# Routing layer of a two-layer conditioned transformer on one core: shared expert parts started two passes earlier, small VectorE steps given to GpSimd

## The reference

```python
# layer 0, pooling
scores = einsum('bsa,a->bs', tanh(hidden @ W1 + b1), v)
p = softmax(where(mask, scores[:, None, :], NEG_INF), -1)
pooled = einsum('bjl,bld->bjd', p, hidden) / mask.sum(-1)[..., None]
# layer 0, routing of the pooled tokens xf
s = softmax(xf @ wg.T)                        # 32 experts in 8 groups
keep_g = the 4 groups with the largest maximum
_, idx = top_k(where(keep_g, s, -inf), 4)
w = take(s, idx);  w = w / (w.sum(-1) + 1e-9)
pos = (cumsum(one_hot(idx), 0) * one_hot(idx)).sum(-1) - 1   # place in the expert
keep = pos < 640
y = scatter_add(w * experts(gather(xf)))
z = (silu(xf @ sw1) * (xf @ sw3)) @ sw2       # the shared expert
x = x + y + z
```

## Time and profile before

| | us |
|---|---|
| median of 3 runs | 1539.36 (1530.76 to 1539.44) |
| profiled execution | 1537.86 |
| its span on the core | 1536.1 |
| TensorE busy in the span | 1402.7 (91%) |
| VectorE busy | 1030.4 (67%) |
| ScalarE busy | 897.8 (58%) |
| GpSimd busy | 654.4 (43%) |

### The profile page before, as it was taken

One profiled execution on the slowest core, in us unless ns is written; L12 is line 12 of the kernel. 1 busy time (PEld: TensorE's weight loads), 2 busy tenths in 40 slices (PEclk: granted clock), 3 DMA queues, 4 the chain that ended last, 5 costly groups with the idle time before them and its releaser, 6 DMA issues.

```text
span 1536.1 us, 27264 instructions
## 1 busy us (share of the span) xinstructions
PE 1402.7 (91%) x9777; PEld 1219.8 (79%) x9777; DVE 1030.4 (67%) x2418; ACT 897.8 (58%) x2092; POOL 654.4 (43%) x624
## 2 busy tenths in 40 slices
PE   7987899999999998789998999998729999999996
PEld 5765799999999997568776776776618998998996
DVE  2998567767777775678887887885435556555552
ACT  5775345545555552268887787788626456455452
POOL 0222344434443414455556666643434445345333
PEclk9997899999999999999999999999759999999998
DMA  5421256666655633557576587575422343234212
GB/s 170 138 83 37 64 152 179 174 163 184 175 169 168 178 98 106 100 96 132 122 141 134 100 131 143 99 123 90 123 85 55 87 108 89 47 92 97 41 22 28
DMA packets 134326, 173.59 MB, mean 113 GB/s; under 512 B 21461, under 2 KB 106272, under 8 KB 134192
## 3 DMA queue, kind: packets, MB, share of 16 engines
q1 hardware_dynamic: 106032, 119.89, 30.4%
q0 software_dynamic: 28160, 51.96, 17.7%
HBM read 107.28 MB, written 42.08 MB: 97 GB/s over the span
## 4 chain that ended last, share of the span: by engine, by line
PE 72%; DVE 9%; issue 6%; DMA 6%; ACT 3%; another core or an unknown queue 2%; POOL 2%; SPq 1%; POOLq 0%; DVEq 0%; ACTq 0%
PE banks L929 45%; PE banks L1437 5%; DMA xe<-pooled,idx 4%; PE banks L1480 4%; PE banks L1533 3%; PE banks L991 3%; PE banks L451 2%; PE banks L1493 2%; PE banks L1454 1%; PE banks L1495 1%; PE banks L1909 1%; PE banks L571 1%; DVE row_at L516 1%; PE banks L1452 1%
## 5 line engine op out<-in xcount | busy, mean ns | idle before, releaser
L929 PE MATMUL banks<-hi_x,hi_w 128*128 128x320 f32 (+1 forms) x832 | 290.7, 349 | 12.1 <-DVE hidden L964 5.2
L929 PE MATMUL banks<-lo_x,hi_w 128*128 128x320 f32 (+1 forms) x832 | 288.1, 346 | 0.0
L929 PE MATMUL banks<-hi_x,lo_w 128*128 128x320 f32 (+1 forms) x832 | 287.6, 346 | 0.0
L929 PE MATMUL banks<-hi_w,hi_h 128*128 128x256 f32 x896 | 261.1, 291 | 2.5 <-DVE X L1018 2.1
L870 POOL DMA_INDIRECT xe<-pooled,idx x160 | 159.2, 995 | 237.4 <-DVE hidden L964 104.3
L929 PE MATMUL banks<-lo_w,hi_h 128*128 128x256 f32 x896 | 253.8, 283 | 0.0
L929 PE MATMUL banks<-hi_w,lo_h 128*128 128x256 f32 x896 | 253.7, 283 | 0.0
L1894 POOL DMA_INDIRECT out<-X,tab x64 | 106.1, 1658 | 190.7 <-DVE X L1997 176.1
L1584 ACT ACTIVATE PN<-banks,smax 128x256 f32<-128x256 f32 (+1 forms) x512 | 180.0, 442 | 12.6 <-DVE smax L1690 12.6
L1410 POOL DMA_INDIRECT got<-done,slot x128 | 126.6, 989 | 133.9 <-DVE smax L1690 70.4
L929 PEld LDWEIGHTS banks<-hi_x,hi_w 128*128 128x128 f32 x832 | 159.9, 192 | 27.3 <-issue 11.0
(11 more groups left out here) (187 smaller groups left out, 2950.7 us busy)
## 6 DMA issues: line engine op xcount, KB each, us to landing
w<-in_L_ffn_w SPq DMA_DIRECT2D x96, 256.0 KB
done<-res SPq DMA_DIRECT2D x32, 640.0 KB
BIG<-in_L_ffn_W SPq DMA_DIRECT2D x16, 1024.0 KB
QS<-parts_qk SPq DMA_DIRECT2D x96, 128.0 KB
KS<-parts_qk SPq DMA_DIRECT2D x96, 128.0 KB
mask<-in_c_masks SPq DMA_DIRECT2D x16, 257.0 KB, 2.8
pooled<-XF SPq DMA_DIRECT2D x16, 256.0 KB, 3.2
WS<-in_L_cond_W SPq DMA_DIRECT2D x16, 256.0 KB
```

What stands on the lines that cost most here:

```text
L929: last = e.matmul(o, a[i], b[j], start=start and k == 0, stop=stop and k == 2, skip_group_check=True)
```

## The change

It does three things. The shared parts' steps stand two passes earlier in the tables of all four engines (`up` of part 0 in TensorE's pass 2 in place of 4, and so on). The second half's one-hot rows (`lane`, half 1) move on VectorE from behind `hit` to the next pass, behind the row maximum `nm` and the `rank` step. And GpSimd takes over from VectorE the pooling's inverse sums (`pool_norm`), the chosen weights (`pool_weigh`) and the running counts (`pool_cum`); with -1 in a new tile `inverse`, the inverse is a power. VectorE's max instruction of the next group and ScalarE's exp of the next group both wait for the chosen weights of the group ahead, which GpSimd now writes. `dve_found` stands at the end of VectorE's list. In layer 1 two loads count on another semaphore; nothing moves there.

```diff
+            if q == 0 and g >= 1 and r.groups:
+                e.wait_ge(r.s_weighted, g)
-        if r.groups:
-            e.tensor_reduce(r.top[:, 0:n], r.tv[:, 0:n, 0:K], AX.X, ALU.add).then_inc(*st.next())
+        if not r.groups:
+            e.reciprocal(r.inv[:, 0:n], r.den[:, 0:n]).then_inc(*st.next())
             yield
             e.wait_ge(st.sem, st.n)
-            e.scalar_tensor_tensor(r.top[:, 0:n], r.den[:, 0:n], 1e-9, r.top[:, 0:n], ALU.mult, ALU.add).then_inc(*st.next())
+            e.tensor_tensor(r.weights[:, t0:t0 + n, :], r.tv[:, 0:n, 0:K], wide(r.inv[:, 0:n], 2, [P, n, K]),
+                            ALU.mult).then_inc(r.s_weighted, 1)
             yield
-            e.wait_ge(st.sem, st.n)
-        e.reciprocal(r.inv[:, 0:n], (r.top if r.groups else r.den)[:, 0:n]).then_inc(*st.next())
-        yield
+
+    def pool_weigh(e, r, g):
+
+        st = pool_steps
+        t0, n = r.tiles(g)
+        e.wait_ge(r.s_hit, g + 1)
+        e.wait_ge(r.s_exp, g + 1)
+        e.tensor_tensor(r.pair[:, 0:n, :], r.tv[:, 0:n, 0:2], r.tv[:, 0:n, 2:4], ALU.add).then_inc(*st.next())
+        e.tensor_scalar(r.inv[:, 0:n], r.den[:, 0:n], 1e-9, None, ALU.mult).then_inc(*st.next())
         e.wait_ge(st.sem, st.n)
-        e.tensor_tensor(r.weights[:, t0:t0 + n, :], r.tv[:, 0:n, 0:K], wide(r.inv[:, 0:n], 2, [P, n, K]),
+        e.tensor_tensor(r.top[:, 0:n], r.pair[:, 0:n, 0], r.pair[:, 0:n, 1], ALU.add).then_inc(*st.next())
+        e.wait_ge(st.sem, st.n)
+        e.tensor_tensor(r.top[:, 0:n], r.top[:, 0:n], r.inv[:, 0:n], ALU.add).then_inc(*st.next())
+        e.wait_ge(st.sem, st.n)
+        e.tensor_tensor(r.inv[:, 0:n], r.top[:, 0:n], inverse[:, 0:n], ALU.pow).then_inc(*st.next())
+        e.wait_ge(st.sem, st.n)
+        e.tensor_tensor(r.weights[:, t0:t0 + n, :], r.tv[:, 0:n, 0:r.K], wide(r.inv[:, 0:n], 2, [P, n, r.K]),
                         ALU.mult).then_inc(r.s_weighted, 1)
-        yield
 
...
-        e.tensor_reduce(r.add[:, :], r.sel[:, 0:n, :].rearrange("p r e -> p e r"), AX.X, ALU.add).then_inc(*st.next())
-        e.wait_ge(st.sem, st.n - 1)
+        placed = st.n
+        if not r.groups:
+            e.tensor_reduce(r.add[:, :], r.sel[:, 0:n, :].rearrange("p r e -> p e r"), AX.X, ALU.add).then_inc(*st.next())
+        e.wait_ge(st.sem, placed)
         e.scalar_tensor_tensor(r.sm[:, 0:n, :], pos, float(r.cap), r.sm[:, 0:n, :], ALU.is_lt, ALU.mult).then_inc(r.s_placed, 1)
+        if not r.groups:
+            e.wait_ge(st.sem, st.n)
+            e.tensor_tensor(r.cum[:, :], r.cum[:, :], r.add[:, :], ALU.add).then_inc(*st.next())
+
+    def pool_cum(e, r, g):
+
+        st, n = pool_steps, r.sizes[g]
+        e.wait_ge(r.s_ranked, g + 1)
+        e.tensor_tensor(r.two[:, 0:2, 0, :], r.sel[:, 0:2, :], r.sel[:, 2:4, :], ALU.add).then_inc(*st.next())
+        e.wait_ge(st.sem, st.n)
+        e.tensor_tensor(r.add[:, :], r.two[:, 0, 0, :], r.two[:, 1, 0, :], ALU.add).then_inc(*st.next())
...
-        ("up", -5, 1), ("mix", 3, 0), ("find", 0, 2), ("mix", 3, 1), ("down", -6, 0), ("find", 0, 3),
-        ("turn", 5, 1), ("turn", 6, 0), ("up", -4, 0), ("turn_back", 3, 0), ("turn_back", 3, 1),
-        ("scores", 4, 1), ("down", -6, 1), ("scores", 5, 0), ("turn_p", 4, 0), ("find", 1, 0))
+        ("up", -3, 1), ("mix", 3, 0), ("find", 0, 2), ("mix", 3, 1), ("down", -4, 0), ("find", 0, 3),
+        ("turn", 5, 1), ("turn", 6, 0), ("up", -2, 0), ("turn_back", 3, 0), ("turn_back", 3, 1),
+        ("scores", 4, 1), ("down", -4, 1), ("scores", 5, 0), ("turn_p", 4, 0), ("find", 1, 0))
     DVE_ROUND0 = (
-        ("split_x", -2, 0), ("scores", 6, 0), ("up", -3, 0), ("logits", 4), ("rank", 3),
-        ("norm", 5, 1), ("choose", 4, 0), ("split_x", -2, 1), ("down", -5, 1), ("slots", 3),
-        ("choose", 4, 1), ("split_h", -3, 0), ("up", -3, 1), ("lane", 3, 0), ("choose", 4, 2), ("choose", 4, 3),
-        ("lane", 3, 1), ("scores", 6, 1), ("down", -4, 0), ("norm", 6, 0), ("split_h", -3, 1), ("choose", 4, 4))
+        ("split_x", 0, 0), ("scores", 6, 0), ("up", -1, 0), ("logits", 4), ("rank", 3), ("lane", 2, 1),
+        ("choose", 4, 0), ("split_x", 0, 1), ("down", -3, 1), ("slots", 3),
+        ("choose", 4, 1), ("split_h", -1, 0), ("up", -1, 1), ("lane", 3, 0), ("choose", 4, 2), ("choose", 4, 3),
+        ("scores", 6, 1), ("down", -2, 0), ("split_h", -1, 1))
     ACT_ROUND0 = (
-        ("mix", 2, 1), ("split_x", -4, 1), ("turn", 4, 1), ("split_h", -6, 1), ("turn", 5, 0),
-        ("turn_back", 2, 0), ("turn_back", 2, 1), ("token", 0, 0), ("token", 0, 1), ("up", -5, 0), ("token", 0, 2),
-        ("split_h", -5, 0), ("weigh", 3, 1), ("turn_p", 3, 0), ("logits", 2), ("token", 0, 3), ("hidden", 4, 1),
-        ("split_x", -3, 0), ("up", -5, 1), ("weigh", 4, 0), ("turn_p", 3, 1), ("hidden", 5, 0), ("mix", 3, 0))
-    POOL_ROUND0 = (("count", 6), ("pick", 6))
+        ("mix", 2, 1), ("split_x", -2, 1), ("turn", 4, 1), ("split_h", -4, 1), ("turn", 5, 0),
+        ("turn_back", 2, 0), ("turn_back", 2, 1), ("token", 0, 0), ("token", 0, 1), ("up", -3, 0),
+        ("split_h", -3, 0), ("weigh", 3, 1), ("turn_p", 3, 0), ("logits", 2), ("token", 0, 2), ("token", 0, 3), ("hidden", 4, 1),
+        ("split_x", -1, 0), ("up", -3, 1), ("weigh", 4, 0), ("turn_p", 3, 1), ("hidden", 5, 0), ("mix", 3, 0))
+    POOL_ROUND0 = (
+        ("pick", 3), ("norm", 5, 1), ("cum", 3), ("count", 4), ("weigh", 4), ("norm", 6, 0))
     SP_ROUND0 = (
         ("mask", 4, 0), ("store", 1, 1), ("store", 2, 0), ("mask", 4, 1))
-    CHOICES = (0, 5, 11, 17, 22, 26)
+    CHOICES = (0, 5, 11, 17, 22)
...
+    def pool_norm(e, b):
+
+        st, i = pool_steps, b % 2
+        e.wait_ge(s_pr, TB * (b + 1))
+        e.wait_ge(s_mask_in[b % NMK], 16 * (b // NMK + 1))
+        if b >= 2:
+            e.wait_ge(s_XF, TB * (b - 1))
+        e.tensor_tensor(psum_[:, i, :], psum_[:, i, :], mask[:, b % NMK, TB * T:], ALU.mult).then_inc(*st.next())
+        e.wait_ge(st.sem, st.n)
+        e.tensor_tensor(pinv[:, i, :], psum_[:, i, :], inverse[:, 0:TB], ALU.pow).then_inc(s_pinv, 1)
...
-            elif step == "norm":
-                e.wait_ge(s_pr, TB * (b + 1))
-                if b >= 2:
-                    e.wait_ge(s_XF, TB * (b - 1))
-                e.tensor_tensor(psum_[:, i, :], psum_[:, i, :], mask[:, b % NMK, TB * T:], ALU.mult).then_inc(*dve_steps.next())
-                e.wait_ge(dve_steps.sem, dve_steps.n)
-                e.reciprocal(pinv[:, i, :], psum_[:, i, :]).then_inc(s_pinv, 1)
...
-                if (g, *d) == (NSH - 1, 1):
-                    dve_found(e)
                 dve_split_h(e, g, *d)
             elif step == "down":
                 dve_down(e, g, *d)
+        dve_found(e)```

Line numbers in the next rows are those of the changed file. **ScalarE, pass 3 of its own table (R = 1).** Here `gate` (L997) is the Silu of `up`, `hi_h` is `split_h`, `pr` is `weigh`, `ex` the router's exp. Before (its numbers L955, L971, L635, L200) the same stretch of the stage had no shared step between two exps until all of the pooling's exps were done:

```order
L653 ACTIVATE XFT<-banks 128x2x256 x2
L523 ACTIVATE lane_at<-lane_at,find 128x512 x2
L955 ACT_TABLE_LOAD
L955 ACTIVATE gate<-banks 128x512
L523 ACTIVATE lane_at<-lane_at,find 128x512
L971 ACTIVATE hi_h<-hidden 128x512
L200 ACT_TABLE_LOAD
L200 ACTIVATE ex,den<-banks,nm 128x32 x4
```

26 lines of the change are left out of this document (19 added, 7 removed).

## The result

| | before | after |
|---|---|---|
| median | 1537.2 us (1530.23 to 1541.39, 20 runs) | 1541.41 us (1536.31 to 1544.96, 20 runs) |
| ratio | | 1.0028, 95% interval 1.0016 to 1.0040 |
| span of the profiled execution | 1536.1 us | 1537.2 us |
| `idx` begins | 167.09 us | 180.02 us |
| experts 2 to 31 (of 0 to 31), from the first transpose of expert 2 to that of expert 31 | 354.4 us | 343.6 us |

The kernel became slower by 0.3%, where I had forecast a gain of 0.2%. The time lies in the range, but two large errors nearly cancel in it: the first stage lost 12.9 us in place of gaining 5.7, and the experts behind it, which I took as unchanged, became 10.8 us shorter.

A forecast was written before the change was run, and what follows sets the result against it. First stage: VectorE paces the quiet passes, then a chain from last `hit` to `idx` counts. `idx` at 161.7 in place of 167.4, -5.7 us, plus 2.5 for a slow half `up`: -3 us, median 1536.4, range 1523 to 1548.

The forecast's parts named there:

- The 0.7 us: First stage, three quiet passes of 13.9 us: the end of group 3's `hit` at 81.5 us, against 82.2.
- My 2.4: GpSimd's chain for the chosen weights: 2.4 us estimated, between bounds of 2.1 and 4.2.
- Passes 1 and 2: ScalarE becomes the bound: First stage: nine table loads in place of three, 7.7 us more; the two passes take 17.9 and 18.9 us.
- third rival: TensorE falls to the lower clock behind waits, passes 1 to 3 pay 4 us each: +6, or 1545; chance 0.2.
- The 2.5 us: TensorE, passes 1 and 2: 2.5 us added for one more half `up` at the lower clock.
- Pass 0: First pass after the quiet ones, taking up weights' splits and part 0's first `split_x`: 15.1 us, `gs` at 5.9.
- Pass 3: TensorE late with the last router product: group 7's `hit` ends at 150.5 against 145.1, shared work costing 5.4 us.
- the tail: From the last `hit` to `idx`, with no `up` in between: 11.2 us in place of 22.3, -11.1 us.
- Everything behind the stage shifts and stays as it is.: Behind the first stage, the experts included: only moved in time, no change in length.
- rival 4: The stage's gain doesn't arrive because the first experts' gathers or weights take longer: no change, 1539; chance 0.03.
- The first (loads in idle time): Table loads fall into ScalarE's idle time, passes 1 to 3 take 15.6 us each: -12.8, or 1526.6; chance 0.17.
- The second (GpSimd's chain at its upper bound): GpSimd's chosen-weights chain takes 4.2 us in place of 2.4: +8.4 on the sum, +5, or 1545; chance 0.13.

The follow-up runs named there:

- One table: The changed kernel with Tanh in place of Silu in the first stage's three shared parts; ratio 0.9961 against the kernel before, `idx` at 170.1 us.
- after again: The changed kernel, unchanged, run a second time; ratio 1.0033 against the kernel before, `idx` at 180.4 us.

## Why the prediction was wrong, point by point

**What held.** The power came at 1.04 us, there are nine loads of 1.28 us after the initial one, and in the quiet passes VectorE's `gs` waits for an exp that waits for GpSimd. The 0.7 us that this was to gain in three quiet passes are not there (H3 at 82.5, forecast 81.5): `w_pick` takes 0.6 us longer beside `row_at`, and the chain has five gaps of 0.08. My 2.4 held 0.3 for gaps that it doesn't name; its terms as written add up to 2.1. The table load begins where the instruction ahead ends, as in the earlier trace rows: `hi_h` from 103.71 to 104.34, load at 104.36, exp at 105.65. The drain that the Trainium skill (ScalarE: Activation LUTs, section What ACT_TABLE_LOAD costs) adds is not in this trace either.

**The step that failed: "Passes 1 and 2: ScalarE becomes the bound".** I put 17.9 and 18.9 us there, from ScalarE's sum and from one walk along VectorE, and the measured ones are 20.2 and 25.0. Both workings took one engine's list as running through. ScalarE was busy 15.17 of 20.18 and 16.40 of 25.02: it stood for 5.0 and 8.6 us, in pass 1 mostly in waits for TensorE, which in turn lost 2.97 and 3.66 us in waits for `prT` behind loads. My walk had the pooling's exps on VectorE's path, not on TensorE's, where the copy `prT`, `mix` and the next `scores` stand behind them. In pass 2 `gs` came 14.6 us behind the `hit` where the walk had 8.5; from `gs` to the next `hit` it took 10.4, as forecast. This is the third rival's mechanism, waits behind table loads and then the lower clock, with its price too low in pass 2: 4 us a pass on top of the forecast, against 2.3 and 6.1. One table removes it and the two passes fall to 16.6 and 17.3. The 2.5 us that I had for one half `up` at the lower clock were 1.6, and the `mix` behind the second wait added 1.6.

**Pass 0: 17.4 for 15.1** (19.1 in some runs). `gs` came 8.2 us behind the `hit`, where I had 5.9: VectorE stood 1.15 us for TensorE's `scores`, and the second `row_at` took 1.89 us beside GpSimd's `pick`, where 0.82 was counted. Where the pass takes 19.1, in after again, that wait is 2.83 us, and it ends within 0.3 us of the time at which it ends in after: TensorE, on which I counted nothing, sets it. It is 19.1 with one table as well, and no load stands in this pass: the loads are no part of it.

**Pass 3: 20.4 for 17.1, and the tail: 14.5 for 11.2.** In pass 3 TensorE is busy 12.39 of 20.38 us: again waits in turn, with two more loads (at 152.1 and 155.8). In the tail the places wait for TensorE's running count 2.88 us behind the last shared part, granted clock 0.76, and `row_at` takes 1.89 us beside GpSimd:

```profile
169.85 0.29 DVE L318 TENSOR_TENSOR sm<-banks,small 128x128 f32<-128x128 f32 x1 [2.88 <-PE banks L310]
...
170.98 1.89 DVE L556 TENSOR_TENSOR row_at<-find_h,parts 128x1280 f16<-128x1280 f16 x1
...
180.02 0.32 DVE L601 TENSOR_SCALAR idx<-banks 128x160 uint32<-128x160 f32 x1 [0.43 <-PE banks L571]
```

Still 7.5 us shorter than before's 22.0. The gain that the step forward was there for is real, and smaller than its price.

The sum of it: 1.0 to H3, 14.0 in passes 0 to 3, 3.3 in the tail make 18.3 us, and `idx` at 180.0 in place of 161.7. (The 161.7 is the end of `idx`, so the miss is 0.3 larger.)

**"Everything behind the stage shifts and stays as it is."** From `idx` to the first `up` it nearly did: 12.9 us after 12.2. The experts did not, by 10.8 us here and 7.4 between the two kernels run again. That the time still fell into my range is luck: the place of `res`, which was no part of the plan, covered most of the stage's loss. No rival had this; rival 4 had the stage's gain lost there, not a loss covered. With `res` off its place, as in before, the changed kernel is at 1.0068 (expected 1.008 to 1.010). That is what its own order costs.

**The rivals.** The first (loads in idle time) is refuted: H5 came at 120.1. The second (GpSimd's chain at its upper bound) is too: the chain from `pair` to the end of `w_pick` took 3.1 us in a quiet pass, 0.7 over the 2.4 and 1.1 under the bound, most of it in `w_pick` beside `row_at`.

## What to carry to other kernels

Moving work forward into a stage whose engines wait for each other has to be priced on every engine of the new place, TensorE's too, and with each wait that the moved step puts on somebody else's path; a function that needs another table than its neighbours costs less for its loads than for what queues behind them. And a tile, however small, moves every tile allocated behind it: before a difference is put down to an order of instructions, compare a stage that the change doesn't touch, and pad the kernel before so that both have the same places.

## What the runs showed of the hardware

- Stores from `res`, rows of 1024 bytes: with `res` at a multiple of 512 bytes 99% of the 1024-byte packets near a store take 46 ns; off it (32, 64 or 480 past one) 25 to 43%, and the mean is 50 to 51 ns against 47. The experts' stage is 2 to 3% shorter, the kernel 0.4 to 0.6%.
- A GpSimd power takes 0.70 us on 128x2 and 1.04 on 128x4, a product on 128x2 0.19, a sum on 128x4 0.20. Beside VectorE's f16 `row_at`, GpSimd's `w_pick` took 0.84 us where it takes 0.22 otherwise; beside GpSimd's `pick` (1.65, alone 1.27) `row_at` took 1.89 where it takes 0.82 otherwise.
- TensorE came out of a wait of 2.97 us at the level of 1.2 GHz (granted clock 0.53) and stayed there for eight products of 512 columns; out of 3.66 us as well, for a whole `mix`. Out of 0.54 us it came at 2.4, and in a quiet pass out of 2.54 us too, so the length of the wait alone doesn't tell the level:

```profile
79.12 1.97 PE L640 MATMUL banks<-X,prT 128*128 128x256 f32 x8 [2.54 <-ACT prT L692]
```
